# One of the 64 row gathers of each step moved from GpSimd to SyncE, row by row

## What is computed

```python
q = (x @ Wq).reshape(b, n, HEADS, DIM) * DIM ** (-0.5)
kv_scores, indices = _pk(x, Wq_pk, pk_keys)      # 16 row numbers and 16 softmax weights per token and head
ind = indices + offsets[None, None, :, None]
k = jnp.einsum('bnhk,bnhkd->bnhd', kv_scores, keys_table[ind])
v = jnp.einsum('bnhk,bnhkd->bnhd', kv_scores, values_table[ind])
sim = jnp.einsum('bihd,bjhd->bhij', q, k)        # then causal softmax
out = jnp.einsum('bhij,bjhd->bhid', attn, v)
out = out.transpose(0, 2, 1, 3).reshape(b, n, HEADS * DIM)
return out @ Wo
```

## Time and profile before

| | |
|---|---|
| median of 3 runs | 10309.92 us (10309.65 to 10334.59) |
| span of the profiled execution | 10308.3 us, from the first to the last instruction |
| POOL busy | 7753.8 us, 75% |
| PE busy | 6307.9 us, 61% |
| DVE busy | 5392.5 us, 52% |
| ACT busy | 1516.6 us, 15% |
| DMA | 1106.38 MB, 107 GB/s over the span |
| granted TensorE clock, mean | 0.779 of full speed |

### The profile page before, as it was taken

How to read it: one execution, slowest core, us unless ns; L and a number is a source line. 1 busy time by engine, 2 the same in 40 slices (tenths; PEclk the granted TensorE clock), 3 DMA queues, 4 the chain that set the end, 5 groups by cost and what they waited for, 6 DMA issues and landing times.

```text
span 10308.3 us, 94047 instructions
## 1 busy us (share of the span) xinstructions
PE 6307.9 (61%) x24864; PEld 5021.6 (49%) x24864; DVE 5392.5 (52%) x21631; ACT 1516.6 (15%) x4051; POOL 7753.8 (75%) x8201
## 2 busy tenths in 40 slices
PE   5666655666566666666656666666566666665666
PEld 4444544544445444454444444444444444544544
DVE  5554555555555555554554545555554555555553
ACT  1111111111111111111111111111111111111111
POOL 6777777777777777777777777777777777777777
PEclk7777777777777777777778777777777777777777
DMA  3333333333333333333333333333333333333333
GB/s 107 105 112 105 105 112 105 112 105 105 112 105 112 105 105 112 105 111 105 105 112 105 111 105 105 112 105 112 105 105 112 105 112 105 105 112 105 106 105 99
DMA packets 420765, 1106.38 MB, mean 107 GB/s; under 512 B 131952, under 2 KB 149744, under 8 KB 420208
## 3 DMA queue, kind: packets, MB, share of 16 engines
q0 software_dynamic: 393216, 1074.27, 36.4%
q1 hardware_dynamic: 27120, 27.46, 0.9%
HBM read 1097.01 MB, written 4.19 MB: 107 GB/s over the span
## 4 chain that ended last, share of the span: by engine, by line
POOL 73%; issue 24%; PE 1%; DVE 1%; POOLq 0%; DMA 0%; ACT 0%; SPq 0%; DVEq 0%
POOL got L232 73%; PE comb_ps L325 1%; DMA got<-in_table,rows 0%; DVE diag L670 0%; DVE onehot L643 0%; DVE rows L647 0%; DVE onehot L640 0%; POOLq L226 0%; POOLq L229 0%; PE score_ps L338 0%; DMA adj_i<-in_adj 0%; POOLq L230 0%; POOLq L227 0%; PE small_ps L353 0%; DVE const_ps L615 0%
## 5 line engine op out<-in xcount | busy, mean ns | idle before, releaser
L232 POOL DMA_INDIRECT got<-in_table,rows x8192 | 7752.0, 946 | 2535.1 <-issue 2489.0
L325 PE MATMUL comb_ps<-got,diag 128*128 128x256 f32 x16384 | 4635.4, 434 | 3273.1 <-DMA got<-in_table,rows 3228.6
L325 PEld LDWEIGHTS comb_ps<-got,diag 128*128 128x128 f32 x16384 | 3460.6, 221 | 4060.5 <-issue 3401.6
L670 DVE TENSOR_TENSOR diag<-const_ps,wts 128x2048 f32<-128x2048 f32 x512 | 1160.9, 2288 | 224.2 <-issue 167.5
L679 DVE CUSTOM_DVE_ANT_0 neg<-score_ps,mask 128x128 f32<-128x128 f32 (+3 forms) x512 | 251.6, 491 | 1929.8 <-PE score_ps L338 1929.8
L699 DVE SCALAR_TENSOR_TENSOR acc<-probT_ps,prob_inv,acc 128x128 f32<-128x128 f32 x448 | 157.2, 351 | 1936.0 <-PE probT_ps L359 1936.0
L393 ACT ACTIVATE keyT<-small_ps 128x128 f32<-128x128 f32 x512 | 141.8, 277 | 2772.7 <-PE small_ps L332 2772.7
L353 PE MATMUL small_ps<-probT,kv 128*128 128x128 f32 x2560 | 468.1, 325 | 87.8 <-ACT probT L393 87.8
L353 PEld LDWEIGHTS small_ps<-probT,kv 128*128 128x128 f32 x2560 | 430.9, 230 | 152.8 <-ACT probT L393 133.2
L647 DVE TENSOR_REDUCE rows<-onehot 128x32 uint32<-128x1600 f32 (+1 forms) x257 | 466.0, 1813 | 27.9
L300 PE MATMUL front_ps<-w_sim,x2nT 128*128 (+1 forms) x1024 | 410.7, 572 | 108.6 <-issue 95.1
(11 more groups left out here) (91 smaller groups left out, 4928.3 us busy)
## 6 DMA issues: line engine op xcount, KB each, us to landing
got<-in_table,rows POOLq DMA_INDIRECT x8192, 2.8
adj_i<-in_adj SPq DMA_DIRECT2D x16, 1024.0 KB, 7.9
x_in<-in_x SPq DMA_DIRECT2D x16, 256.0 KB, 3.6
out<-fin SPq DMA_DIRECT2D x16, 256.0 KB, 3.5
wqpk_sb<-in_wqpk_t SPq DMA_DIRECT2D x1, 512.0 KB, 10.8
keys_sb<-in_keys_t SPq DMA_DIRECT2D x1, 512.0 KB, 14.4
wq_sb<-in_wq SPq DMA_DIRECT2D x1, 512.0 KB, 14.0
wo_sb<-in_wo SPq DMA_DIRECT2D x1, 512.0 KB, 15.2
```

The lines of the kernel that those rows point to most:

```text
L232: pool.indirect_dma_start(out=got[t][:, k, :], out_offset=None, in_=table, in_offset=bass.IndirectOffsetOnAxis(ap=rows[par][:, t * TOPK + ...
L325: mm = pe.matmul(comb_ps[t % 2][:, 0:2 * D], diag[t % 2][:, k, :], got[t][:, k, :], start=(k == 0), stop=(k == TOPK - 1))
L670: dve.tensor_tensor(diag[t % 2][:, :, :], ident_ps.unsqueeze(1).broadcast_to([P, TOPK, P]), wts[par][:, t, :].unsqueeze(2).broadcast_to([P ...
```

## The change

The last gather of each step (tile 3, k = 15) is no longer issued by POOL. SP fetches its 128 rows one by one: for partition p it loads the row number `rows[par][p, 63]` from SBUF into a register (`value_load`, with bounds from 0 to 131071) and issues a DMA of that one row, 1 KB, into partition p of a buffer of its own, `got_last[par]`. Two such buffers alternate by step. `fetched[par]` counts 16 for each of the 128 transfers; PE waits for all of them, 2048, right before the matmul of k = 15, and clears the semaphore. SP waits before a fetch for all four tiles of `rows_ready` of that step, and for `combined` of the step that used the buffer before, two steps back. The gathers of tile 3 count 15 instead of 16, in the last tile's last quarter 3 instead of 4.

On SP the loads of the next batch and the store now stand between fetches: the loads of the next batch ahead of the fetch of the batch's head 0, the store of a batch behind the fetch of the next batch's head 0, and the landing of that store is awaited there. Nothing else is changed.

```diff
+    got_last = [sb(f"got_last{i}", [P, 2 * D]) for i in range(2)]
...
+    fetched = [sem(f"fetched{i}") for i in range(2)]
...
-        with sp.Fori(0, B - 1) as b:
+
+        def fetch(s, par, reuse=True):
+            sp.wait_ge(rows_ready, s * T + T)
+            sp.sem_inc(held, 1)
+            if reuse:
+                sp.wait_ge(combined, s * T - T)
+                sp.sem_inc(held, 1)
+            for p in range(P):
+                row = sp.value_load(rows[par][p:p + 1, T * TOPK - 1:T * TOPK], min_val=0, max_val=H * ROWS - 1)
+                sp.dma_start(got_last[par][p:p + 1, :], table[bass.ds(row, 1), :]).then_inc(fetched[par], 16)
+
+        def more(b):
+            with sp.Fori(0, H // 2 - 1) as i:
+                fetch(b * H + i * 2 + 2, 0)
+                fetch(b * H + i * 2 + 3, 1)
+
+        def load_next(b):
             sp.wait_ge(x_used, b + 1)
             load_x(b + 1)
             sp.wait_ge(adj_cast, b + 1)
             load_adj(b + 1)
-            sp.wait_ge(fin_ready, (b + 1) * T)
-            store(b)
-            sp.wait_ge(out_stored, (b + 1) * 16)
+
+        def store_last(b):
+            sp.wait_ge(fin_ready, b * T)
+            store(b - 1)
+            sp.wait_ge(out_stored, b * 16)
             sp.sem_inc(fin_free, 1)
+
+        load_next(0)
+        fetch(0, 0, reuse=False)
+        fetch(1, 1, reuse=False)
+        more(0)
+        with sp.Fori(0, B - 2) as i:
+            load_next(i + 1)
+            fetch((i + 1) * H, 0)
+            store_last(i + 1)
+            fetch((i + 1) * H + 1, 1)
+            more(i + 1)
+        fetch((B - 1) * H, 0)
+        store_last(B - 1)
+        fetch((B - 1) * H + 1, 1)
+        more(B - 1)
         sp.wait_ge(fin_ready, B * T)
...
-                for k in range(TOPK):
+                for k in range(TOPK - 1 if t == T - 1 else TOPK):
                     pool.indirect_dma_start(
...
                 end = last and t == T - 1
+                n = (TOPK - 1 if t == T - 1 else TOPK) * 16
                 if k0 == 0 and not end:
-                    pe.wait_ge(gathered[t], s * (TOPK * 16) + TOPK * 16)
+                    pe.wait_ge(gathered[t], s * n + n)
...
                     if end and k % (TOPK // QUARTERS) == 0:
-                        pe.wait_ge(gathered_end[k * QUARTERS // TOPK], TOPK // QUARTERS * 16)
-                    mm = pe.matmul(comb_ps[t % 2][:, 0:2 * D], diag[t % 2][:, k, :], got[t][:, k, :],
+                        q = k * QUARTERS // TOPK
+                        pe.wait_ge(gathered_end[q], (TOPK // QUARTERS - q // (QUARTERS - 1)) * 16)
+                    row_by_row = t == T - 1 and k == TOPK - 1
+                    if row_by_row:
+                        pe.wait_ge(fetched[par], P * 16)
+                        pe.sem_clear(fetched[par])
+                    mm = pe.matmul(comb_ps[t % 2][:, 0:2 * D], diag[t % 2][:, k, :],
+                                   got_last[par][:, :] if row_by_row else got[t][:, k, :],
                                    start=(k == 0), stop=(k == TOPK - 1))
```

## The result

The changed kernel takes 20951.91 us (20938.95 to 20954.06, 3 runs), the kernel before 10309.92 us: 2.03 times as long (95% interval 2.029 to 2.035). The forecast of 18,830 us was 10% short, inside its range of 10,800 to 22,000 us.

The account below looks back on a forecast made before the run. POOL's gathers were taken to bound the kernel before, SP's row fetches the changed one: 65 us start, 16384 rows of 1.14 us (18,678 us), 73 us between batches, 16 us end, giving 18,830 us; range 10,800 to 22,000 us.

Parts of the forecast that it names:

- What bounds before, and what the gather is worth: POOL's gathers bound the kernel before; dropping 128 of 1.2508 us each gains 160.1 us if SP keeps up.
- The threshold of 0.611 us a row: On SP: the most a row may take for SP to keep up with POOL's 63 gathers, 78.8 us a step.
- break-even rival: On SP: a row between 0.611 and 0.63 us leaves the time within 0.3%; chance 0.02.
- The price of a row, 1.14 us: On SP: 0.57 us for loading the row number plus 0.57 us for the row DMA, not overlapped.
- The distance of 0.57 us: On SP, from the issue of `x` to that of `adj` in the old trace; taken as the row DMA's price.
- The skill's figure: Floor of about 600 ns for a `tensor_load`; by it a row would be 1.17 us, the kernel some 19,320 us.
- The sum around it: Around SP's rows: start 65 us, 4.9 us between batches, end 16 us; rows always ready, the store's landing hidden.
- Costed at nothing: PE's extra semaphore wait and clearing, the shorter gather count, the small transfers' packets, and fetching SP's longer code: 0 us.
- SP keeps up: Rival on SP: load up to 0.04 us, row at most 0.611 us, POOL still bounds, 10,150 us; chance 0.11.
- cheap load of 78 to 166 ns: Rival on SP: load like a small DVE instruction, row 0.65 to 0.74 us, 10,800 to 12,280 us; chance 0.17.
- the row come to 1.52 us: Rival on SP: load, check and register work cost a full gather, 24,990 us; chance 0.06 for above 1.33 us a row.
- What I said that the profile would show: POOL's share about 41%, waiting over 60 us a step for `combined`; SP's queue the chain; PE's wait 60 to 100 us.

Follow-up runs that it names:

- 56 rows: The changed kernel, but SP fetches only 56 of the 128 rows of a step and PE waits for 56 transfers: 10152.22 us, ratio 0.985 to the kernel before.
- the version with a line: The changed kernel with a step's row numbers first brought into one partition, eight per load, no bounds check: 10149.29 us, ratio 0.985 to the kernel before.

## Why the prediction was right

- **What bounds before, and what the gather is worth.** Right: 56 rows and the version with a line both give 155 to 158 us of the 160.1.
- **The threshold of 0.611 us a row.** Not tried at the point itself, but held on both sides: rows of 0.55 us (56 x 1.26 / 128) and 0.52 us (66 us for 128) are hidden, 0.71 us (72 x 1.26 / 128) is not. The break-even rival was worked out wrongly: from 0.611 to 0.63 us a row the time would go from 10,150 to 10,480 us, 1.5% under to 1.6% over, and only rows within 0.002 us of 0.621 stay within 0.3%. Nothing hangs on it at 1.24 us.
- **The price of a row, 1.14 us.** This is the term that was mis-sized: 1.242 us, and 1.273 us with everything around it. Its parts were off in both directions. The load with its gap is 0.53 us where I had 0.57. That it came so close is luck: I had it from the difference between a gather on POOL and an issue on SP, and no run shows that a gather's time splits like that. The other five instructions with their gaps are 0.71 us where I had 0.57. Of these the issue of the DMA is 255 ns, where I didn't expect much under 373 ns: size, or the shape of the transfer, does count for something. The check of the bounds, for which I let a met wait of some 0.1 us stand, is two instructions and 0.26 to 0.28 us. And every small instruction brings 0.03 to 0.05 us of gap: of 1.24 us, 0.25 us are gaps. The distance of 0.57 us held four instructions (an issue, a met wait, two for the address), and a row has five besides the load.
- **The skill's figure.** The Trainium skill, page "DMA: Bandwidth & Descriptors", section "Latency and other measured facts", has a floor of about 600 ns for a `tensor_load`. The runs here show less: 0.27 us behind another load, 0.43 us behind a semaphore wait, 0.50 to 0.53 us behind a DMA. The measurement decides.
- **The sum around it.** Start 67.5 us (65 forecast), end 16.1 us (16). Rows ready in time: SP waited for them only once. The store's landing cost 27.6 us in all, 1.8 us a batch. Between two fetches there are 1.7 us more than a row on average, 220 us in all, where I had 73 us: about half of it stands at the turns of SP's loops (next point).
- **Costed at nothing.** PE's extra wait, the DMA packets (two for each row, not 17): hidden, as said. The fetching of SP's code did show, if that is what these gaps are: the packets of the instruction queue went from 290 to 1151, and the row distance is 0.3 us longer about every 21 rows, 0.02 us a row or 284 us in all. At each of 45 turns of SP's loops SP stands 2.4 us behind the branch, where the short loop before had 0.12 us, so some 100 us more. I had allowed 256 us for the turns alone, in the range and not in the sum, and nothing for the rows within a fetch. That code is fetched in these gaps is inferred from the packets, not tested.
- **The rivals.** "SP keeps up" failed by a factor of two at its point of decision. The cheap load of 78 to 166 ns was not seen: the lowest median is 0.27 us, and even with it the other parts of the row would still make about 1 us. Nor did the row come to 1.52 us.
- **What I said that the profile would show.** Right: POOL at 36% (41% forecast), SP's queue as the chain, PE's wait once a step and 90 us long. Not quite: POOL's wait for `combined` is 58 us a step on average, 49 to 63 us, where I had said over 60. Not foreseen: POOL also waits 3402.1 us for row numbers, 27 us a step, while DVE in its turn waits for PE; it is hidden behind SP.

With all terms measured the sum closes: 16383 distances of 1.242 us are 20,348 us, the longer gaps within fetches 284 us, what stands between fetches over a row 220 us, and both ends 84 us, together 20,936 us of the 20,937 us of span. Of the 2,105 us by which my 18,832 us fell short, 1,671 us are the price of a row, 284 us the gaps within fetches, and 147 us what stands between them.

## What to carry to other kernels

An idle engine is not a free one: before work is moved to it, divide its period by the number of items, and compare this with all instructions per item, register work, checks and gaps included, not with the two that the code names. Here 78.8 us over 128 rows were 0.62 us (0.611 us with the other work of SP), and six small instructions took 1.24. The same move pays once several items share an instruction and the check is gone (eight numbers a load, no run-time check), and a run with fewer items shows cheaply on which side of the threshold one is.

## What the runs showed of the hardware

- A register load from SBUF on SP takes 0.27 us behind another load, 0.43 us behind a semaphore wait with no DMA issue near, and 0.50 to 0.53 us right behind a DMA issue, although issues in a row come every 0.29 us. A load of eight numbers takes 0.78 us behind a DMA and 0.70 us behind a semaphore instruction. Why the load depends on what stands ahead, no run here shows.
- The issue of a row DMA of 1 KB has a record of 255 to 260 ns on SP when it is the first behind a load, and of 225 ns behind another row's issue.
- The mean granted TensorE clock fell from 0.779 to 0.636 of full speed in the changed kernel, in which PE stands still for 90 us at a time; of the two levels, 1.2 and 2.4 GHz, the higher one has 27% of the time instead of 56%. From 4998 to 5040 us, with PE busy for 22.0 of 42 us, the granted clock is 0.83 of full speed; from 5040 to 5130 us, with 8.2 of 90 us, it is 0.50. PE's busy time rose from 6307.9 to 6709.1 us for the same instructions, without any effect on the end.
- On two of the three chips of the experiments every kernel was slower, the kernel before by 1.47, with POOL's gathers at 946 to 949 ns as elsewhere. In stretches of 12 to 65 us most of SP's instructions took 0.7 us with a gap of 0.7 us behind them, and ACT at times stood idle for 10 us and more with a releaser that the trace can't name. The kernels with more instructions on SP mostly lost more (the kernel without the check took 23,743 us there, while by its parts 16,500 us were expected), but the kernel before, with next to nothing on SP, lost 4,800 us as well. What it is, these runs leave open.
